# Expert products from float32r high and low parts, with weights loaded by halves into three sets

## The reference

```python
x = x + xattn(layernorm(x), ctx, ctx, w_q, w_kv, w_concat)      # 16 x 128 tokens, 256 wide, 16 heads
y = layernorm(x)
attn_out = layer_norm(y) * attn_nw + attn_nb
combine, dispatch = top1_gate(attn_out, wg, capacity=256)        # 8 experts, 256 places each
dispatched = einsum('sec,sm->ecm', dispatch, attn_out)           # 8 x 256 x 256
h = gelu(einsum('ecm,emi->eci', dispatched, inter_w) + inter_b)  # 256 -> 1024
expert_out = einsum('eci,eim->ecm', h, output_w) + output_b      # 1024 -> 256
moe_out = einsum('sec,ecm->sm', combine, expert_out)
res = gelu(attn_out @ res_inter_w + res_inter_b) @ res_output_w + res_output_b
out = x + y + res * coef[:, :1] + moe_out * coef[:, 1:]          # coef = softmax(attn_out @ res_coef)
```

## Time and profile before

| what | value |
|---|---|
| median of 3 runs | 447.14 us (445.47 to 448.82) |
| profiled execution | 447.72 us, of which 446.0 us are the span of the profile |
| PE busy, share of the span | 86% |
| DVE, ACT, POOL busy | 32%, 38%, 34% |
| mean granted PE clock | 0.92 of full speed |
| up of expert 0 starts | 320.8 us |
| last down of expert 7 ends | 437.4 us |

### The profile page before, as it was taken

One profiled execution on the slowest core, in us unless ns is written; L12 is line 12 of the kernel. 1 busy time (PEld: TensorE's weight loads), 2 busy tenths in 40 slices (PEclk: granted clock), 3 DMA queues, 4 the chain that ended last, 5 costly groups with the idle time before them and its releaser, 6 DMA issues.

```text
span 446.0 us, 5656 instructions
## 1 busy us (share of the span) xinstructions
PE 381.6 (86%) x1978; PEld 292.7 (66%) x1978; DVE 142.2 (32%) x461; ACT 167.6 (38%) x325; POOL 153.2 (34%) x219
## 2 busy tenths in 40 slices
PE   4767777778998788988988988889999899999992
PEld 2435245555676476576576566678888788888881
DVE  3263424532354354363364263241101010101020
ACT  3213334345255435534536525552243223332310
POOL 4322313218156238247238035265002121212122
PEclk9757666986999999998999999999999999999998
DMA  7678650230022462381411410085122775581212
GB/s 203 189 193 233 228 134 2 76 79 24 23 72 77 125 234 71 94 272 51 114 35 61 104 37 12 21 294 165 47 68 64 196 235 166 128 251 12 25 18 29
DMA packets 51331, 49.78 MB, mean 112 GB/s; under 512 B 4764, under 2 KB 48488, under 8 KB 51304
## 3 DMA queue, kind: packets, MB, share of 16 engines
q1 hardware_dynamic: 48232, 45.21, 33.2%
q0 software_dynamic: 3072, 4.21, 5.2%
HBM read 33.65 MB, written 15.63 MB: 111 GB/s over the span
## 4 chain that ended last, share of the span: by engine, by line
PE 65%; DMA 10%; ACT 8%; DVE 7%; issue 5%; POOL 2%; SPq 2%; DVEq 0%; POOLq 0%; ACTq 0%
PE mbank L776 20%; PE ubank L612 18%; PE mbank L612 11%; DMA drow<-dispatched 8%; PE mbank L607 4%; PE pbank L697 4%; ACT p L847 3%; PE sbank L665 3%; PE sbank L687 3%; DVE smax L977 3%; PE pbank L706 2%; DVE core L1021 2%; ACT h L890 1%; DMA wq_raw<-in_L_xattn_w_q 1%; ACT oT L791 1%
## 5 line engine op out<-in xcount | busy, mean ns | idle before, releaser
L890 ACT ACTIVATE h<-ubank,vecT 128x256 f32<-128x256 f32 x128 | 53.7, 471 | 131.7 <-PE ubank L612 131.7
L776 PE MATMUL mbank<-w2r,h 128*128 128x256 f32 x256 | 64.1, 390 | 0.5 <-ACT h L890 0.5
L612 PE MATMUL ubank<-ao,w1r 128*128 128x256 f32 x256 | 62.7, 393 | 0.0
L776 PE MATMUL mbank<-w2e,h 128*128 128x256 f32 x256 | 60.8, 379 | 0.0
L580 POOL DMA_INDIRECT out_rows<-yrow,rowid x16 | 24.8, 1548 | 103.7 <-DVE yrow L1097 73.5
L612 PE MATMUL ubank<-ao,w1e 128*128 128x256 f32 x256 | 60.0, 379 | 0.0
L776 PEld LDWEIGHTS mbank<-w2r,h 128*128 128x128 f32 x256 | 48.4, 194 | 12.8 <-issue 5.3
L612 PEld LDWEIGHTS ubank<-ao,w1r 128*128 128x128 f32 x256 | 49.4, 197 | 6.6
L612 PEld LDWEIGHTS ubank<-ao,w1e 128*128 128x128 f32 x256 | 48.5, 190 | 6.6
L776 PEld LDWEIGHTS mbank<-w2e,h 128*128 128x128 f32 x256 | 48.2, 190 | 6.3
L977 DVE TENSOR_REDUCE smax<-sbank 128x4 f32<-128x512 f32 x64 | 41.9, 685 | 26.5 <-PE sbank L665 26.2
(11 more groups left out here) (123 smaller groups left out, 438.1 us busy)
## 6 DMA issues: line engine op xcount, KB each, us to landing
w1e<-in_L_ffn_inter_w SPq DMA_DIRECT2D x8, 1024.0 KB, 4.9
w2e<-in_L_ffn_output_w SPq DMA_DIRECT2D x8, 1024.0 KB, 8.4
qstack<-dram_q SPq DMA_DIRECT2D x16, 384.0 KB, 4.6
dram_q<-qpart SPq DMA_DIRECT2D x8, 384.0 KB, 2.5
dispatched<-zrow SPq DMA_DIRECT2D x4, 516.0 KB, 5.4
drow<-dispatched SPq DMA_DIRECT2D x8, 258.0 KB, 8.3
xs<-in_x SPq DMA_DIRECT2D x8, 256.0 KB, 4.6
ctxs<-in_ctx SPq DMA_DIRECT2D x8, 256.0 KB, 4.7
```

The lines of the kernel that those rows point to most:

```text
L612: last = nc.tensor.matmul(dst, w[kc], v[kc], start=(kc == 0), stop=(kc == len(w) - 1))
L776: last = nc.tensor.matmul(b[:, 0:D], h[:, n % 2, f, t * P:(t + 1) * P], w2[:, f, :], start=(f == 0), stop=(f == FC - 1))
L890: nc.scalar.activation(h[:, n % 2, f, :], place["up", n, c][:, j, :], ACT.Gelu_apprx_tanh, bias=vecT[:, col:col + 1]).then_inc(sem("gelu_d ...
```

## The change

Each expert operand X is split into a high part (X written as float32r) and a low part (X minus high, written as float32r), and a product becomes three float32r products: high x high, high x low, low x high. The residual MLP and attention stay as they were.

- ACT makes the high parts of the rows (`aoh`), of the first weights (`w1h`, step `ws1`, four quarters of 128 x 512) and of `h` (`hh`, one copy for each c).
- DVE makes the low parts of the rows (`aol`) and of `h` (`hl`), and both parts of the second weights (`w2h`, `w2l`, step `ws2`, four quarters).
- POOL makes the low part of the first weights (`w1l`).
- The low parts take the place of the float32 data in the same memory, so that a set holds `w1e` and then `w1l`. The sets go from four to three, high parts have two places each, `drow` and `outb` four places instead of eight.
- Loads are split: `w1load(e)` waits for `up` of expert e - 3, `w2load(e)` for `down` of it, and each has a place in the order of its own.
- `EXPERT` has new numbers; in PE's list `down` of expert e - 1 now stands whole behind `up` of expert e, with `ein` of the next between its two tiles.

```diff
-    SETS = 4
+    SETS = 3
+    EIN = 4
+    Q = 4
@@ EXPERT
-        "period": 17.22, "up": [-2.35, 2.53, 4.67, 9.02],
-        "down": [17.16, 18.79, 20.45, 21.34, 23.58, 25.85, 26.32, 28.49], "ein": [9.47], "first": [-3.51],
+        "period": 12.0, "up": [0.0, 1.45, 2.9, 4.35], "down": [17.9, 18.6, 19.3, 20.0, 20.7, 21.4, 22.1, 22.8],
+        "ein": [4.0], "first": [-3.51], "ws1": [-17.0, -15.0, -13.0, -11.0], "ws2": [0.2, 2.2, 4.2, 6.2],
+        "w1load": [6.5], "w2load": [23.9],
@@ SP
+            def w1load(e):
+                if e >= SETS:
+                    sp.wait_ge(sem("up_done"), C2 * (U + e - SETS + 1))
...
+            def w2load(e):
+                if e >= SETS:
+                    sp.wait_ge(sem("down_done"), T * (U + e - SETS + 1))
...
+                if e >= EIN:
+                    sp.wait_ge(sem("y_ready"), T * (e - EIN + 1))
@@ POOL
+            def split(e, q):
+                pool.wait_ge(sem("w1_high"), Q * e + q + 1)
+                w = quarter(w1e[e % SETS], q)
+                pool.tensor_tensor(quarter(w1l[e % SETS], q), w, quarter(w1h[e % 2], q).bitcast(f32), ALU.subtract).then_inc(sem("w1_low"), 1)
@@ PE, up
+                    e = n - U
+                    if c == 0:
+                        pe.wait_ge(sem("ao_low"), e + 1)
+                        pe.wait_ge(sem("w1_low"), Q * (e + 1))
...
+                        wh, wl = chunks(w1h[e % 2], f), chunks(w1l[e % SETS], f)
+                        ah, al = chunks(aoh[:, e % 2, :, :]), chunks(aol[:, n % NAO, :, :])
+                        last = product(b[:, j, :], wh + wh + wl, ah + al + ah)
@@ PE, down
+                        pe.wait_ge(sem("w2_low"), Q * (e + 1))
+                if n >= U and t == 0:
+                    pe.wait_ge(sem("h_low"), C2 * e + q + 1)
...
+                        nc.tensor.matmul(b[:, 0:D], hi, wh, start=(f == 0), stop=False)
+                        nc.tensor.matmul(b[:, 0:D], hi, wl, start=False, stop=False)
+                        last = nc.tensor.matmul(b[:, 0:D], lo, wh, start=False, stop=(f == FC - 1))
@@ ACT
+                    copy(aoh[:, n % 2, :, :], ao[:, n % NAO, :, :]).then_inc(sem("ao_high"), 1)
+            def split(e, q):
...
+                copy(quarter(w1h[e % 2], q), quarter(w1e[e % SETS], q)).then_inc(sem("w1_high"), 1)
@@ ACT, up
+                    act.wait_ge(sem("gelu_done"), 2 * (i + 1))
+                    copy(hh[:, n % 2, 2 * c:2 * c + 2, :], h[:, n % 2, 2 * c:2 * c + 2, :]).then_inc(sem("h_high"), 1)
@@ DVE
+                V.tensor_tensor(aol[:, (U + e) % NAO, :, :], a, aoh[:, e % 2, :, :].bitcast(f32), ALU.subtract).then_inc(sem("ao_low"), 1)
+            def split(e, q):
...
+                V.tensor_copy(quarter(w2h[e % 2], q), w).then_inc(sem("w2_high"), 1)
+                dve.wait_ge(sem("w2_high"), Q * e + q + 1)
+                V.tensor_tensor(quarter(w2l[e % SETS], q), w, quarter(w2h[e % 2], q).bitcast(f32), ALU.subtract).then_inc(sem("w2_low"), 1)
+            def up(n, c):
...
+                dve.wait_ge(sem("h_high"), i + 1)
+                V.tensor_tensor(hl[:, n % 2, 2 * c:2 * c + 2, :], a, hh[:, n % 2, 2 * c:2 * c + 2, :].bitcast(f32), ALU.subtract)\
+                    .then_inc(sem("h_low"), 1)
```

More of the change, by code:

```diff
@@ L9, in xattn_moe_ffn_kernel @@
     f32 = mybir.dt.float32
+    f32r = mybir.dt.float32r
     bf16 = mybir.dt.bfloat16
@@ L170, in xattn_moe_ffn_kernel @@
             add(own + phase, "down", U + e, i // 4, i % 4)
+        for kind in ("ws1", "ws2"):
+            for q, phase in enumerate(EXPERT[kind]):
+                add(own + phase, kind, e, q)
         if e + SETS < E:
-            add(own + EXPERT["period"] + 12.5, "wload", e + SETS)
+            for kind in ("w1load", "w2load"):
+                add(own + EXPERT[kind][0], kind, e + SETS)
     add(1e6, "end")
@@ L208, in xattn_moe_ffn_kernel @@
         core = sb("core", [P, 2, T, ROW], f32)
-        ao = sb("ao", [P, NAO, KC, UT], f32)
-        h = sb("h", [P, 2, FC, UT], f32)
+        first = ex.enter_context(ExitStack())
+        ao = sb("ao", [P, NAO, KC, UT], f32, first)
+        h = sb("h", [P, 2, FC, UT], f32, first)
+        w1e = [sb(f"w1e{i}", [P, KC, F], f32, first) for i in range(2)]
+        w2e = [sb(f"w2e{i}", [P, FC, D], f32, first) for i in range(2)]
+        first.close()
+        aol = sb("aol", [P, NAO, KC, UT], f32r)
+        hl = sb("hl", [P, 2, FC, UT], f32r)
+        w1l = [sb(f"w1l{i}", [P, KC, F], f32r) for i in range(2)]
+        w2l = [sb(f"w2l{i}", [P, FC, D], f32r) for i in range(2)]
         yrow = sb("yrow", [P, 2, T, D], f32)
@@ L261, in xattn_moe_ffn_kernel, with quarter @@
         att.close()
-        w1e += [sb(f"w1e{i}", [P, KC, F], f32) for i in range(2, SETS)]
-        w2e += [sb(f"w2e{i}", [P, FC, D], f32) for i in range(2, SETS)]
-        drow = sb("drow", [P, E, T, ROW], f32)
+        last = ex.enter_context(ExitStack())
+        w1e += [sb(f"w1e{i}", [P, KC, F], f32, last) for i in range(2, SETS)]
+        w2e += [sb(f"w2e{i}", [P, FC, D], f32, last) for i in range(2, SETS)]
+        last.close()
+        for i in range(2, SETS):
+            w1l.append(sb(f"w1l{i}", [P, KC, F], f32r))
+        for i in range(2, SETS):
+            w2l.append(sb(f"w2l{i}", [P, FC, D], f32r))
+        w1h = [sb(f"w1h{i}", [P, KC, F], f32r) for i in range(2)]
+        w2h = [sb(f"w2h{i}", [P, FC, D], f32r) for i in range(2)]
+        hh = sb("hh", [P, 2, FC, UT], f32r)
+        aoh = sb("aoh", [P, 2, KC, UT], f32r)
+        drow = sb("drow", [P, EIN, T, ROW], f32)
         rowid = sb("rowid", [P, E, T], u32)
-        outb = sb("outb", [P, E, D], f32)
+        outb = sb("outb", [P, EIN, D], f32)
+        def quarter(w, q):
+            return w[:, :, :].rearrange("p k f -> p (k f)")[:, 512 * q:512 * q + 512]
         def weights(n):
@@ L387, in wload @@
                     sp.wait_ge(sem("x1_ready"), U)
[L388 to L395, removed]
+                w1load(e)
+                w2load(e)
             def k_spill(u):
```

104 lines of the change are left out of this document (74 added, 30 removed).

## The result

The changed kernel takes 468.59 us (median of 3 runs, 468.37 to 469.77) against 447.14: a ratio of 1.047, with a 95% interval of 1.040 to 1.054. The forecast was slower, 458.5; it was slower by 21.5 us, not 11. The profiled execution has a span of 467.7 us against 446.0.

A forecast was written before the change was run, and what follows sets the result against it. PE was taken to bound the experts' part; its 26 us gain would turn into about 20 us waiting for rows, 8 for DVE, 4 for ACT and 6 of clock: 458.5 us against 447.72, 454 to 464 (stated range 446 to 472).

The forecast's parts named there:

- the wait for rows: PE before each next expert's rows: rows come 5.8 us after up, PE idle about 8 us once, 3.1 us four times.
- rival D: DVE's and POOL's subtractions hold each other up 2.6 us per period; period 16.4, total 467.5 us; chance 0.12.
- What bounded the kernel before: Experts' part: PE, busy without a break at 14.6 us per expert; the SP queue next behind it.
- The price of a float32r product: Experts' products on PE: 0.110 us each with load hidden, 96 per expert; a gain of 3.2 us per expert.
- rival B: Experts' products on PE: a float32r product costs 0.216 us (float32 record width or unhidden loads); 513 us; chance 0.05.
- rival C: Row loads on the SP queue: drow lands 2.7 us after issue, not behind weights; not slower, 443.5 us; chance 0.13.
- The period of experts 2 to 5: Wait for rows 5.8, turning them 3.1, up 6.1: 15.0 us each, clock loss of 1.2 charged separately.
- The period of experts 6 and 7: No first weights ahead of rows; DVE's chain to ytmp binds: 14.3 us from up to up.
- A: PE's granted clock stays up despite idle stretches, removing the 6.0 us clock charge: 452.5 us; chance 0.20.
- The copy of 128 x 512: DVE's plain copy in its chain: taken as 0.5 us, the middle of 0.35 to 0.63.
- the tail: After the last up: down(6) and down(7) tiles, 11.5 us, then 8.6 us from last matmul to the end.
- Hidden work: POOL's subtractions for the first weights, 5.2 us per expert: hidden in every period but the first.

The follow-up runs named there:

- both edits: Changed kernel with expert rows placed 6 us earlier in SP's list, and POOL's subtraction cut to 8 columns (high part multiplied twice): 439.48 us, ratio 0.992.

## Why the prediction was right, and where its sizes were off

The direction and the wait for rows were right. The size was not: the forecast's own interval, 454 to 464, was missed, and 468.59 lies in the stated range only because that range went up to 472 for rival D, which had been given 12%. D's 467.5 is the nearest of the five forecasts. It is also too low by its own terms (14.3 + 2.6 is 16.9 and not 16.4), so its nearness is in part luck.

**What bounded the kernel before** was right, as the experiment with all subtractions on DVE and the splits spread shows: with PE the bound again, an expert takes 12.5 us instead of 14.6.

**The price of a float32r product.** Taken 0.110, measured 0.118: in `up` of expert 0, two products start every 0.24 us.

```profile
319.22 0.40 PE L656 MATMUL ubank<-aol,w1h 128*128 128x256 f32 x2
319.45 0.40 PE L656 MATMUL ubank<-aoh,w1l 128*128 128x256 f32 x2
319.69 0.40 PE L656 MATMUL ubank<-aoh,w1h 128*128 128x256 f32 x2
```

96 x 0.118 = 11.3 us, so PE's gain is 2.5 us an expert and not 3.2. One record each: rival B is out, and with it the rule of the Trainium skill (TensorE: Matmul & The Clock Gate, Part 3, "The mechanism") as the prediction took it, that a load overlaps only if it goes to other rows; the same section has a load into the background weight buffer pulled ahead too. The trace shows that loads over all rows do overlap: alone a load takes 0.111 and a pass of 256 columns 0.108 (estimated from the bf16 rows there), and together they start every 0.118.

**The wait for rows** was right in place and size. From the end of `up` of expert 2 (SP's issue at 360.26) to the turning of expert 3's rows (365.97) went 5.7 us; forecast 5.8. `drow` landed 5.2 us after its issue (median), so rival C is out: it wanted 2.7. The first load was issued at 326.31 instead of 328.3, and `up` of expert 1 began at 335.99 instead of 337.2, although the units' part ended 3 us earlier than counted.

**The period of experts 2 to 5.** Forecast 15.0 and 1.2 for the clock; measured 16.8, 17.2, 17.2 and 18.8 from the end of one `up` to the end of the next. In the second (377.46 - 360.26) the clock cost more: PE lost 1.7 us in tile 1 of `down` and the transposes, all of it on the path, 0.4 us went to `ytmp`, and the rest to the slower product. In the fourth, half clock held from the transposes over the whole of tile 1:

```profile
400.30:407.20 6.90, 6.39 (x29) 6.02 (x30) 2.61 (x7) 3.21 (x6) 4.10 (x3) 0.51 0.16 19
```

That is about 3.2 us lost (half of the 6.39 that PE was busy) instead of 1.7.

**The period of experts 6 and 7.** This is the term of the sum that was most mis-sized: 14.3 forecast, 17.4 measured (437.51 - 420.13). The step "four times (0.69 + 0.5 + 0.06 + 0.69), then `ytmp`" is right in kind, and DVE does bind there. Its copy took 0.42, less than taken, and behind each other subtractions start every 0.60, which gave back about 0.8 us. What was missing is the collision, 2.6 us at the first `hl` (3.25 instead of 0.69), and the clock, for which the forecast charged nothing here: tile 1 and the hand-over took 4.4 us (437.51 to 441.96) instead of 3, at a granted clock of 0.64. The collision had been rival D, 12%, with 2.6 us. So D was true, and A (clock stays up) was not; the forecast counted clock, in five other places, but no collision. The Trainium skill (SBUF — State Buffer, "SBUF: two separate sides") has DVE and GpSimd take one pair of ports in turn, held for a whole instruction by whichever starts first, if both have SBUF inputs. The trace agrees that one stands while the other works. It goes further in that a DVE subtraction stood still over two POOL instructions, 3.5 us, and by the recorded starts it is not always the first that goes on: the longest `hl` (3.75 us) starts at 391.68, before POOL's pair at 391.77, and the `w2l` above at 364.85, before the pair at 365.39 (starts on POOL are rough). That ports are the cause, rather than something else that the two engines share, no run here can tell; that POOL's subtractions are, the two kernels without them do. I gave D a small chance for want of a row, though D's operations were exactly the ones that the change adds.

**The copy of 128 x 512** took 0.42 us, where the forecast took 0.5 out of 0.35 to 0.63. The 3.4 us that the prediction gives for a copy of 0.35 do not follow from its terms: four copies shorter by 0.15 are 0.6 us in each of two periods, and as much again in the tail.

**Hidden work.** "POOL's subtractions are hidden in every period but the first" was the wrong sentence. They are hidden as to POOL's own time, but not as to what they do to DVE. POOL itself was not held up: its pair beside the standing `hl` takes 3.10 us, and the pair at 369.37, where DVE was idle for most of the time, 3.09.

**The sum.** Forecast span 457.4, measured 467.7. The experts' part was to take 136.8 (457.4 - 320.6) and took 150.2. Of these 13.4 us, about 5 are the periods of experts 2 to 5 (69.9 us against 4 x 16.2) and 6.5 those of experts 6 and 7 (34.5 against the 28.0 of the prediction, whose own terms give 28.3). The other 2 lie in the first two experts; `up` of expert 1 lasted 7.5 us, the first 3 of them at half clock, instead of 6.1. The tail is as forecast, 20.0 against 20.1.

## What to carry to other kernels

When a step is split into parts on several engines, price the chain that each part lengthens and not the engines' shares: here the same 11 us of DVE work per expert, in another order, made the kernel 16 us slower. When two waits end at nearly the same time, each experiment on one of them alone will say that it costs little (5 and 11 us here, 30 together), so take both away before judging either. And before giving GpSimd elementwise work beside VectorE, see what VectorE does at that moment: here two subtractions of 1.3 us there held up one of 0.69 us for 2.6 to 3.1 us.

## What the runs showed of the hardware

- A VectorE subtraction of two SBUF operands that took 0.69 us alone lasted 3.3 to 4.2 us beside two GpSimd subtractions that began within 0.6 us of it, and the GpSimd pair was no longer for it (3.10 us against 3.09). A VectorE copy with one operand was caught too: beside one GpSimd subtraction (341.07, 1.28 us) it took 1.52 instead of 0.42.
- A float32r product of 128 x 128 by 128 x 256 is one record, 0.118 us from start to start at 2.4 GHz; with 128 columns 0.112. At 1.2 GHz both are at 0.21 (256 columns: 336.59 to 338.30 us of the changed kernel, eight products; granted clock 0.50). So, if the load is what sets the 0.112, it slows with the clock as well. Two neighbouring rows of the kernel with half the columns, at a granted clock of 0.50, (338.17 - 337.74) / 2:

```profile
337.74 0.63 PE L656 MATMUL ubank<-aoh,w1h 128*128 128x128 f32 x2
338.17 0.63 PE L656 MATMUL ubank<-aol,w1h 128*128 128x128 f32 x2
```

- In the changed kernel every wait of 2.9 to 3.5 us was followed by a stretch at half clock. One of 3.06 us in the kernel without POOL's subtraction was not (348.88). Waits of 2.1 us were followed by one every second time (all subtractions on DVE, splits as the change had them), and waits of 1.2 us never (granted clock 1.00 from 340 to 420 us with both edits). So the length of a wait alone did not decide it here.
